# Fetching eight of the sixteen token pairs later, from another queue, in a fused early-fusion kernel

## The chip, the cores and the metric

The kernel runs on one core of one Trainium2 chip. The metric is the device time of one execution in microseconds (us), from three runs. A span is the time between the first and the last instruction of one profiled execution.

## The reference: what is computed

```python
h = tok(x)                                  # 32 images: 36 patches x 768 @ W_lin + b, class token, positions
h = concatenate([h, txt], axis=1)           # 37 + 128 = 165 tokens of width 256 per image
h = h + attn(layernorm(h))                  # 16 heads of 16, causal, every 4th key masked out
h = h + ffn(layernorm(h))                   # RMS norm, router over 8 experts, each takes the
                                            # top 660 of 5280 tokens, 256 -> 1024 gelu -> 256,
                                            # weighted, summed back, divided by the gate sums
```

The softmax subtracts a row maximum, so every score is computed twice: once to find the maximum of each query's row, and once, transposed, for the exponentials. All of it is float32; the products that need it are split into a high part and a low part (`q_hi`, `q_lo`).

## The kernel before, in words

There are three stages: attention over 32 images (until about 480 us), a search for the experts' thresholds, and eight experts. The change touches the first alone.

**Residual rows.** `H` holds all tokens in SBUF, as 16 pairs of images, 112 partitions x 768 floats (336 KB) each. `load_pair(queue, p)` fetches pair `p` with its text rows from the input `h0`; `place_cls` copies the class rows and `move_embedded(m)` the 36 patch rows of image `m` into it, once the load has landed. Loads are counted in five groups (`HP`: pairs 0; 1, 2; 3 to 5; 6 to 10; 11 to 15), and `place_cls(i)` waits for the whole of group `i`. Three pairs (0 to 2) are fetched by SyncE (SP) and thirteen by ScalarE (ACT): 3 to 6 at the start, 7 behind the first normalisation (L718), 8 to 15 in the rounds -3 to -1 (L732, L739).

**Rounds.** The five engines' programs are written by hand, each in its own order, and meet at semaphores. `ROUNDS` counts b from -4 to 33. In round b image b+2 gets queries, keys and values (`queries`, `keys`, `values`, L856 to L883), image b+1 its row maxima (`row_scores` L885, `row_max` L1288), image b its scores, exponentials and mix of values. The rounds before 0 are the ramp: TensorE (PE) runs them as `early_rounds` (L991), where the embedding products `embed(g)` (L842) stand between the first images' work.

**Between the engines.** ACT copies the queries out of PSUM as `q_hi` (L668); VectorE (DVE) makes `q_lo` and `k_lo` (`low_q`, `low_k`, L1277). Then SP packs an image (`pack`, L355): three copies of queries into `Qp` and six of keys into `Kp`, SBUF to SBUF, nine DMAs, all on SP's queue. `row_scores(n, 0)` on PE waits for all nine (`qk_packed`). Five row maxima later PE transposes them, DVE copies them (`copy_mT`, L1304), SP sends them into `Qp` (`pack_max`, L372), and `key_scores` (L924) may start. DVE is in order: in round -2 it makes the statistics of pair 1 (`ln1_stats_of(1)`, L1246), which wait for that pair's patch rows to land, and then `low_q(0)` and `low_k(0)`.

Of the kernel before, what the change touches and what calls it, by code (L numbers as in the profile page):

```python
# [53 lines left out]
NPAIR = B // 2  # L54
# [6 lines left out]
SMALL = 65  # L61
SK = 28
XP = ((0, 1), (1, 2), (2, 4), (4, 7), (7, NG))
HP = ((0, 1), (1, 3), (3, 6), (6, 11), (11, NPAIR))


# [59 lines left out]
def build(nc, xT, wl, h0, addrows, clsrows, minus, watt, vecs, rowv, w1, w2, const_f, const_b, out):  # L126
    ctx = ExitStack()
    with ctx:  # L128
# [135 lines left out]
        def bank(i):  # L264
            return ps_all[:, i, :]
# [4 lines left out]

        x_in = [sem(f"x_in{i}") for i in range(len(XP))]
        h_in = [sem(f"h_in{i}") for i in range(len(HP))]
# [58 lines left out]
        def load_x(queue, i):  # L331
            cols = slice(KF * XP[i][0] * GB * NP, KF * min(B, XP[i][1] * GB) * NP)
            queue.dma_start(xT_s[:, cols], xT[:, cols]).then_inc(x_in[i], 16)

        def load_pair(queue, p):
            i = [first <= p < last for first, last in HP].index(True)
            queue.dma_start(H4[0:HROWS, p], h0[:, p * RT:(p + 1) * RT, :]).then_inc(h_in[i], 16)


        @block.sync  # L340
        def _(sp):
            def place_cls(i):
                a, z = HP[i]
                sp.wait_ge(h_in[i], 16 * (z - a))
                sp.dma_start(H4[0:1, a:z, 0, :], cls_s[a:z, 0, :]).then_inc(cls_moved[i], 16)
                sp.dma_start(H4[T - A:T - A + 1, a:z, 1, :], cls_s[a:z, 0, :]).then_inc(cls_moved[i], 16)

            def move_embedded(m):
                g, j = divmod(m, GB)
                n, u = divmod(m, 2)  # L350
                p = 1 + u * (T - A)
                sp.wait_ge(emb_ready, g + 1)
                sp.dma_start(H4[p:p + NP, n, u, :], emb[j * NP:(j + 1) * NP, g, :]).then_inc(moved[n], 16)

            def pack(n):  # L355
                i, h = n % 3, n % 2
                if n >= 3:
                    sp.wait_ge(st_done, 4 * n - 8)
                else:
                    sp.wait_ge(pinit_done, (3, 5, 6)[n])  # L360
                sp.wait_ge(q_ready, n + 1)
                for row, src in enumerate((q_hi, q_hi, q_lo)):
                    sp.dma_start(Qp[32 * row:32 * row + 32, i, :, :].bitcast(F32), src[:, h, :, :].bitcast(F32)).then_inc(qk_packed[i], 16)
                sp.wait_ge(k_ready, n + 1)
                for row, src in enumerate((k_hi, k_lo, k_hi)):
                    for w in range(2):
                        sp.dma_start(Kp[32 * row + HD * w:32 * row + HD * w + HD, i, :, w, :].bitcast(F32),
                                     src[64 * w:64 * w + 64, h, :, :].bitcast(F32)).then_inc(qk_packed[i], 16)

            def pack_max(n):  # L370
                sp.wait_ge(mT_ready, n + 1)
                sp.dma_start(Qp[MROW:MROW + 2, n % 3, :, :].bitcast(F32), mT[0:NH, n % 2, :].bitcast(F32))\  # L372
                  .then_inc(m_packed[n % 3], 16)

            def store_h(p):
                sp.wait_ge(resid_ready, RT * p + RT)
                rows = out.rearrange("b t d -> (b t) d").rearrange("(n r q) d -> n q r d", r=RT, q=A)
                sp.dma_start(rows[p], H4[0:A, p]).then_inc(h_stored, 16)

            def store_xn(p):  # L380
                sp.wait_ge(xn2_ready, RT * p + RT)
                rows = xn_rows.rearrange("(n r q) d -> n q r d", r=RT, q=A)
                sp.dma_start(rows[p], xn2[0:A, p % 2]).then_inc(xn_stored[p % 2], 16)

            load_x(sp, 0)
            sp.dma_start(add_s[0:GB * NP], addrows).then_inc(add_in, 16)
            sp.dma_start(cls_s[:, :, :], clsrows).then_inc(add_in, 16)
            load_pair(sp, 0)
            load_x(sp, 2)
            load_x(sp, 3)  # L390
            load_pair(sp, 1)
            load_pair(sp, 2)
            load_x(sp, 4)

            for b in ROUNDS:
                n, u = divmod(b, 2)
                if 1 <= b < B - 6:
                    for i, (first, _) in enumerate(HP):
                        if b + 6 == 2 * first:
                            place_cls(i)  # L400
                    move_embedded(b + 6)
                if 0 <= b + 2 < B:
                    pack(b + 2)
                if b == -1:
                    place_cls(2)
                    for m in (4, 5, 6):
                        move_embedded(m)
                if 0 <= b + 1 < B:
                    pack_max(b + 1)
                if u == 1 and 0 <= n - 1 < NPAIR:  # L410
                    store_h(n - 1)
                if u == 1 and 0 <= n - 1 < NPAIR:
                    store_xn(n - 1)


            sp.wait_ge(h_stored, 16 * NPAIR)
            for e in range(2):
                sp.dma_start(W1[:, e, :, :], w1[e].rearrange("(k p) f -> p k f", p=128)).then_inc(w1_in[e], 16)
                sp.dma_start(W2[:, e, :, :], w2[e].rearrange("(k p) d -> p k d", p=128)).then_inc(w2_in[e], 16)
            def weights(e, u):  # L420
                sp.wait_ge(w1_split, KD * e - KD)
                apart(sp)
                sp.dma_start(W1[:, u, :, :], w1[e].rearrange("(k p) f -> p k f", p=128)).then_inc(w1_in[u], 16)
                sp.wait_ge(w2_split, KFF * e - KFF)
                apart(sp)
                sp.dma_start(W2[:, u, :, :], w2[e].rearrange("(k p) d -> p k d", p=128)).then_inc(w2_in[u], 16)

            with sp.Fori(1, NE // 2) as it:
                for u in range(2):
                    weights(2 * it + u, u)  # L430
            sp.wait_ge(scattered, 16 * NA * NE)
# [208 lines left out]
        def _(act):  # L640
# [83 lines left out]
            for b in ROUNDS:  # L724
                n, u = divmod(b, 2)
                if 0 <= b + 2 < B:
                    copy_q(b + 2)
                if 0 <= b < B:
                    exps(b, 0)
                if 0 <= b + 2 < B:  # L730
                    copy_k(b + 2)
                for p in {-3: (8, 9), -2: (10, 11), -1: (14, 15)}.get(b, ()):  # L732
                    load_pair(act, p)
                if 0 <= b < B:
                    exps(b, 1)
                if u == 0 and 0 < n + 2 < NPAIR:
                    ln1_apply(n + 2)
                if b == -2:
                    load_pair(act, 12)  # L739
                    load_pair(act, 13)  # L740
                if u == 1 and 0 <= n - 1 < NPAIR and b != B - 1:
                    ln2_apply(n - 1)
                if 0 <= b + 2 < B:
                    copy_v(b + 2)
                if 0 <= b < B:
                    exps(b, 2)
                if u == 1 and n + 2 < NPAIR:
                    copy_xnT(n + 2)
                if 0 <= b < B:
                    exps(b, 3)  # L750
                if b == B - 1:
                    ln2_apply(n - 1)
                if u == 1 and 0 <= n - 1 < NPAIR:
                    copy_xn2T(n - 1)
# [476 lines left out]
        def _(dve):  # L1231
# [6 lines left out]
            def embedded(g):  # L1238
                n = min(GB, B - g * GB) * NP
                dve.wait_ge(emb_mm, g + 1)  # L1240
                dve.tensor_tensor(emb[0:n, g, :], bank(g % 4)[0:n, 0:D], add_s[0:n, 0, :], ALU.add)\
                   .then_inc(emb_ready, 1)
# [39 lines left out]
            def low_q(n):  # L1282
                low_parts(n, bank(6), bq_s, q_hi, q_lo, TE, q_hi_ready, q_ready)

            def low_k(n):
                low_parts(n, bank(7), bk_s, k_hi, k_lo, S, k_hi_ready, k_ready)
# [36 lines left out]
            def round_of(b):  # L1323
                n, u = divmod(b, 2)
                has_q, has_r, has_s, has_p = -2 <= b < B - 2, -1 <= b < B - 1, 0 <= b < B, 0 <= n - 1 < NPAIR
                if b == -4:
                    embedded(1)
                if u == 0 and n + 2 < NPAIR:
                    ln1_stats_of(n + 2)
                if u == 1 and has_p:  # L1330
# [21 lines left out]
                    embedded(10)  # L1352
                if has_r:
                    row_max(b + 1, 0)
                if has_q and b != -1:
                    low_q(b + 2)
                if has_r:
                    row_max(b + 1, 1)
                if has_q and b != -1:
                    low_k(b + 2)  # L1360
                if has_r:
                    row_max(b + 1, 2)
# [367 lines left out]
```

## Time and profile before

| | |
|---|---|
| median of 3 runs | 842.74 us (842.41 to 844.98) |
| the profiled execution: time, span | 846.83 us, 844.9 us |
| PE busy | 743.7 us, 88% of the span |
| DVE, ACT, POOL busy | 567.9, 397.1, 383.2 us |
| chain that ended last: PE, DVE | 34%, 4% |
| DMA over the span | 82.37 MB, 97 GB/s |

PE is by far the busiest engine. The page's 40 slices of the span (21 us each) show where it is not: in the first (6 tenths), around 480 to 550 us, where the search runs on DVE, and at the end. The queue named q1 carries the DMAs that SP issues and q10 those of ACT; each DMA, from either queue, is spread over the same 16 DMA engines. "Idle before, releaser" names what ended an engine's idle time, and the time "to landing" of a DMA runs from its issue to the semaphore that tells of its end.

### The profile page before, as it was taken

How to read it: one execution, taken by the hardware profiler on the slowest of the kernel's cores; microseconds unless marked ns; L12 is line 12 of the kernel's file. 1: busy time of each engine (PE TensorE's matmuls, PEld its weight loads, DVE VectorE, ACT ScalarE, POOL GpSimd, SP SyncE). 2: the span in 40 equal slices, each digit the busy share in tenths (PEclk: the TensorE clock that was granted, in tenths of full speed). 3: DMA queues.
4: the chain of work that ended last, by engine and by line, in shares of the span. 5: the costliest groups of instructions: out<-in, count | busy, mean ns of one | idle time of the engine just before them, and what ended most of it. 6: DMA issues, size and time to landing. Idle time of an engine off the chain costs nothing. (4 is left out here: it accounts for less than half of the span.)

```text
span 844.9 us, 18782 instructions
## 1 busy us (share of the span) xinstructions
PE 743.7 (88%) x6840; PEld 673.4 (80%) x6840; DVE 567.9 (67%) x1343; ACT 397.1 (47%) x858; POOL 383.2 (45%) x534
## 2 busy tenths in 40 slices
PE   6959999999999999999998511389999999999994
PEld 4848888888888888888887411289999999999994
DVE  1326767767767768767666377876787787887461
ACT  0305445545445455455442256045647467375470
POOL 4214455455455455465453324213645437356334
PEclk9979999999999999999999655579999999999998
DMA  9975477475675665575651342002344443443122
GB/s 308 248 127 78 62 122 114 93 100 94 96 123 108 94 94 97 103 123 99 98 83 55 97 156 100 17 17 83 45 132 93 89 139 54 128 99 38 33 29 32
DMA packets 80583, 82.37 MB, mean 97 GB/s; under 512 B 35705, under 2 KB 73575, under 8 KB 80236
## 3 DMA queue, kind: packets, MB, share of 16 engines
q1 hardware_dynamic: 65964, 62.21, 37.3%
q0 software_dynamic: 11840, 11.12, 8.2%
q10 hardware_dynamic: 2688, 7.85, 3.6%
q8 instruction: 55, 0.90, 0.5%
q14 instruction: 36, 0.29, 0.1%
HBM read 34.59 MB, written 16.22 MB: 60 GB/s over the span
## 5 line engine op out<-in xcount | busy, mean ns | idle before, releaser
L626 POOL DMA_INDIRECT out<-r_arena x48 | 80.3, 1672 | 116.7 <-DVE r_arena L1591 104.7
L1298 DVE TENSOR_REDUCE mx<-ps_all 128x4 f32<-128x504 f32 (+1 forms) x160 | 104.9, 668 | 26.3 <-PE ps_all L901 24.9
L530 POOL TENSOR_SCALAR_AFFINE_SELECT r_arena<-r_arena 126x660 f32<-126x660 f32 x128 | 97.0, 768 | 52.1 <-ACT r_arena L690 52.1
L690 ACT ACTIVATE r_arena<-ps_all 126x660 f32<-126x660 f32 x128 | 92.2, 720 | 56.9 <-PE ps_all L924 55.5
L1309 DVE RECIPROCAL r_arena<-ps_all 128x165 f32<-128x165 f32 x64 | 76.1, 1189 | 57.5 <-PE ps_all L939 57.5
L901 PE MATMUL ps_all<-Kp,Qp 96*65 96x56 f32 (+1 forms) x512 | 92.4, 297 | 0.0
L1613 DVE TENSOR_TENSOR hT_lo<-r_arena,hT_hi 128x330 fp32r<-128x330 f32 x128 | 63.2, 500 | 41.8 <-ACT r_arena L803 41.6
L613 POOL DMA_INDIRECT xe<-xn_rows,r_arena x48 | 60.6, 1263 | 62.1 <-issue 35.7
L924 PE MATMUL ps_all<-Qp,Kp 98*126 98x166 f32 x512 | 84.3, 287 | 2.9 <-ACT r_arena L690 2.9
L801 ACT ACTIVATE hT_hi<-ps_all,vec_s 128x330 fp32r<-128x330 f32 x128 | 68.8, 538 | 37.7 <-PE ps_all L1166 36.4
L1166 PE MATMUL ps_all<-xeT_hi,W_hi 128*128 128x330 f32 x256 | 82.8, 323 | 1.8 <-DVE xeT_lo L1605 1.1
L1166 PE MATMUL ps_all<-xeT_lo,W_hi 128*128 128x330 f32 x256 | 81.9, 320 | 0.0
L1166 PE MATMUL ps_all<-xeT_hi,W_lo 128*128 128x330 f32 x256 | 81.6, 319 | 0.0
L1186 PE MATMUL ps_all<-hT_hi,W_hi 128*128 128x330 f32 x256 | 81.5, 319 | 0.0
L1186 PE MATMUL ps_all<-hT_hi,W_lo 128*128 128x330 f32 x256 | 80.6, 315 | 0.0
L1186 PE MATMUL ps_all<-hT_lo,W_hi 128*128 128x330 f32 x256 | 80.4, 314 | 0.0
L668 ACT ACTIVATE q_hi<-ps_all,vec_s 128x166 fp32r<-128x166 f32 x64 | 22.0, 395 | 122.8 <-PE ps_all L862 122.8
L924 PEld LDWEIGHTS ps_all<-Qp,Kp 98*126 98x126 f32 x512 | 68.8, 190 | 8.2 <-ACT r_arena L690 6.5
L901 PEld LDWEIGHTS ps_all<-Kp,Qp 96*65 96x65 f32 (+1 forms) x512 | 68.4, 170 | 5.6
L803 ACT ACTIVATE r_arena<-ps_all,vec_s 128x330 f32<-128x330 f32 x128 | 67.9, 530 | 0.0
L898 PE MATMUL ps_all<-cb 128*128 128x392 bf16 (+1 forms) x160 | 55.6, 347 | 13.4 <-DMA Kp<-k_hi 9.2
L939 PE MATMUL ps_all<-r_arena,V 126*32 126x165 f32 x1024 | 62.5, 316 | 1.1 <-POOL r_arena L530 1.0
(182 smaller groups left out, 1712.5 us busy)
## 6 DMA issues: line engine op xcount, KB each, us to landing
H<-w SPq DMA_DIRECT2D x16, 1024.0 KB, 5.7
Qp<-q_hi SPq DMA_DIRECT2D x64, 166.0 KB, 3.9
Kp<-k_hi SPq DMA_DIRECT2D x128, 63.0 KB, 4.1
Qp<-q_lo SPq DMA_DIRECT2D x32, 166.0 KB, 4.6
out<-H SPq DMA_DIRECT2D x16, 330.0 KB
xn_rows<-r_arena SPq DMA_DIRECT2D x16, 330.0 KB
H<-h ACTq DMA_DIRECT2D x13, 336.0 KB, 11.4
Kp<-k_lo SPq DMA_DIRECT2D x64, 63.0 KB, 4.0
```

The lines of the kernel that those rows point to most:

```text
L530: pool.affine_select(PT[0:S, g, :, :], PT[0:S, g, :, :], [[0, 4], [STEP - 1, T]], ALU.is_ge, 0.0, base=STEP - 2, channel_multiplier=-STEP) ...
L626: pool.indirect_dma_start(rows_out, bass.IndirectOffsetOnAxis(tok[0:A, e % NTB, a:a + 1], 0), yw[0:A, a, :], None, bounds_check=NTOK - 1, ...
L690: act.activation(PT[0:S, g, :, :].rearrange("p (k h) t -> p k h t", k=2), pair[:, :, :, 0:T], ACT.Exp, scale=float(HD) ** -0.5).then_inc(e ...
L801: act.activation(hT_hi[:, f, j * HALF:(j + 1) * HALF], bank(n % 4)[:, 0:HALF], ACT.Gelu, bias=b1_s[:, e, f:f + 1]).then_inc(gelu_done, 1)
L803: act.activation(h_raw[:, n % 4, :], bank(n % 4)[:, 0:HALF], ACT.Gelu, bias=b1_s[:, e, f:f + 1]).then_inc(gelu_done, 1)
L901: mm = pe.matmul(dst[0:rows, 2 * j * cols:2 * (j + 1) * cols].rearrange("p (w s) -> p w s", w=2), Qp[0:MROW, q, h, at_row:at_row + rows], ...
L924: mm = pe.matmul(dst[0:S, j * TE:(j + 1) * TE], Kp[0:MROW + 2, q, h, g % 2, :], Qp[0:MROW + 2, q, h, :], start=(j == 0), stop=(j == 1), sk ...
L1166: mm = pe.matmul(bank(n % 4)[:, 0:HALF], w[:, k, f * 128:(f + 1) * 128], x[:, k, cols], start=(i == 0), stop=(i == len(terms) - 1))
L1186: mm = pe.matmul(bank(4 + c)[:, 0:HALF], w[:, f, c * 128:(c + 1) * 128], h[:, f, cols], start=(i == 0), stop=(i == len(terms) - 1))
L1298: dve.tensor_reduce(dst, src, AX.X, ALU.max).then_inc(max_ready, 1)
L1309: dve.reciprocal(rS[:, c, :], bank(2 + c)[:, T:2 * T]).then_inc(rs_sum, 1)
L1613: dve.tensor_tensor(hT_lo[:, f, cols], h_raw[:, n % 4, :], hT_hi[:, f, cols].bitcast(F32), ALU.subtract).then_inc(h_ready, 1)
```

## The change

Two things change. Pairs 8 to 15 are no longer fetched by ACT in the rounds -3 to -1, but by SP: pair 8 in round -1, pairs 9 to 15 in the even rounds 0, 2, ... 12, each behind that round's `pack_max`. And on DVE `low_q(0)` and `low_k(0)` stand ahead of the statistics of pair 1. No wait is added or taken away.

```diff
+LATE = 8
@@ SyncE, in the loop over ROUNDS
                 if 0 <= b + 1 < B:
                     pack_max(b + 1)
+                if b == -1:
+                    load_pair(sp, LATE)
+                if u == 0 and 0 <= n and LATE + 1 + n < NPAIR:
+                    load_pair(sp, LATE + 1 + n)
                 if u == 1 and 0 <= n - 1 < NPAIR:
                     store_h(n - 1)
@@ ScalarE, in the loop over ROUNDS
-                for p in {-3: (8, 9), -2: (10, 11), -1: (14, 15)}.get(b, ()):
-                    load_pair(act, p)
...
-                if b == -2:
-                    load_pair(act, 12)
-                    load_pair(act, 13)
@@ VectorE, round_of(b)
+                if b == -2:
+                    low_q(0)
+                    low_k(0)
                 if u == 0 and n + 2 < NPAIR:
                     ln1_stats_of(n + 2)
...
-                if has_q and b != -1:
+                if has_q and b >= 0:
                     low_q(b + 2)
...
-                if has_q and b != -1:
+                if has_q and b >= 0:
                     low_k(b + 2)
```

DVE's program around round -2 (`st`, `mv`: the statistics of pair 1; `emb`: the embedding's rows), before:

```order
L1241 TENSOR_TENSOR emb<-ps_all,add_s 108x256
L1246 BN_STATS st<-H 110x6 x3
L1250 BN_AGGR mv<-st 110x2 x3
L1277 SCALAR_TENSOR_TENSOR q_lo<-ps_all,vec_s,q_hi 128x166 x2
L1277 SCALAR_TENSOR_TENSOR k_lo<-ps_all,vec_s,k_hi 128x126 x2
L1241 TENSOR_TENSOR emb<-ps_all,add_s 108x256 x2
```

and after:

```order
L1241 TENSOR_TENSOR emb<-ps_all,add_s 108x256
L1277 SCALAR_TENSOR_TENSOR q_lo<-ps_all,vec_s,q_hi 128x166 x2
L1277 SCALAR_TENSOR_TENSOR k_lo<-ps_all,vec_s,k_hi 128x126 x2
L1246 BN_STATS st<-H 110x6 x3
L1250 BN_AGGR mv<-st 110x2 x3
L1241 TENSOR_TENSOR emb<-ps_all,add_s 108x256 x2
```

The four instructions of the low parts have passed the six of the statistics.

SP's program from the end of round -1 to round 1 (`Qp<-mT` is `pack_max`, the other `Qp` and `Kp` rows are `pack`, `H<-emb` is `move_embedded`), before:

```order
L353 DMA H<-emb 36x256 x3
L372 DMA Qp<-mT 2x8x166
L363 DMA Qp<-q_hi 32x4x332 x2
L363 DMA Qp<-q_lo 32x4x332
L367 DMA Kp<-k_hi 16x8x126 x2
L367 DMA Kp<-k_lo 16x8x126 x2
L367 DMA Kp<-k_hi 16x8x126 x2
L372 DMA Qp<-mT 2x8x166
L353 DMA H<-emb 36x256
```

and after (all lines are one further down):

```order
L354 DMA H<-emb 36x256 x3
L373 DMA Qp<-mT 2x8x166
L338 DMA H<-h 112x768
L364 DMA Qp<-q_hi 32x4x332 x2
L364 DMA Qp<-q_lo 32x4x332
L368 DMA Kp<-k_hi 16x8x126 x2
L368 DMA Kp<-k_lo 16x8x126 x2
L368 DMA Kp<-k_hi 16x8x126 x2
L373 DMA Qp<-mT 2x8x166
L338 DMA H<-h 112x768
L354 DMA H<-emb 36x256
```

A load (`H<-h`) now stands behind a `pack_max` and ahead of the next round's work, here twice, and once more in each of the even rounds 2 to 12. On ACT the eight loads are gone from between the first activations, whose order stays.

## Rows read from the trace of the kernel before

**Rows 1.** Waits of PE, 0 to 110 us: us in total, times, longest.
```profile
PE ps_all L898 <- DMA Kp<-k_hi: 9.2, 1, 9.2
...
PE ps_all L881 <- DVE q_lo L1277: 0.7, 1, 0.7
```

**Rows 2.** Timeline of PE: start, us, line, operation, idle before and releaser.
```profile
44.50 2.75 PE L842 MATMUL ps_all<-r_arena 128*72 128x256 f32 x12
56.41 0.49 PE L898 MATMUL ps_all<-cb 128*128 128x392 bf16 x1 [9.16 <-DMA Kp<-k_hi]
56.44 0.88 PE L901 MATMUL ps_all<-Kp,Qp 96*128 96x252 f32 x2
...
65.28 0.88 PE L924 MATMUL ps_all<-Qp,Kp 98*126 98x166 f32 x4
...
88.50 0.34 PE L898 MATMUL ps_all<-cb 128*128 128x392 bf16 x1
88.54 0.54 PE L901 MATMUL ps_all<-Kp,Qp 96*128 96x252 f32 x2
```

**Rows 3.** Timeline of ACT and DVE, 28 to 45 us.
```profile
30.47 0.69 ACT L668 ACTIVATE q_hi<-ps_all,vec_s 128x166 fp32r<-128x166 f32 x2 [2.58 <-PE ps_all L862]
...
31.62 0.36 ACT L674 ACTIVATE k_hi<-ps_all,vec_s 128x126 fp32r<-128x126 f32 x1
...
32.54 1.08 DVE L1246 BATCH_NORM_STATS2 st<-H 110x6 f32<-110x256 f32 x3 [2.77 <-DMA H<-emb]
...
33.86 0.65 DVE L1277 SCALAR_TENSOR_TENSOR q_lo<-ps_all,vec_s,q_hi 128x166 fp32r<-128x166 f32 x2
...
37.58 0.36 ACT L681 ACTIVATE V<-ps_all 126x256 f32<-126x256 f32 x1
```

**Rows 4.** Timeline of SP, 30 to 90 us: start and length of the issues.
```profile
34.60 1.33 SPq L363 DMA_DIRECT2D Qp<-q_hi  x2
...
63.13 0.69 SPq L372 DMA_DIRECT2D Qp<-mT  x1
...
74.05 0.67 SPq L372 DMA_DIRECT2D Qp<-mT  x1
...
79.24 1.95 SPq L363 DMA_DIRECT2D Qp<-q_hi  x2
```

**Rows 5.** Landing of the last DMA that packs image 0, issued at 39.92 us.
```profile
DMA to landing us min/median/max: 16.4/16.4/16.4
```

**Rows 6.** The page's DMA issues: KB each, median us to landing.
```profile
Kp<-k_hi SPq DMA_DIRECT2D x128, 63.0 KB, 4.1
...
H<-h ACTq DMA_DIRECT2D x13, 336.0 KB, 11.4
```

**Rows 7.** DMA queues, 33.2 to 52.6 us: packets, MB, share of 16 engines.
```profile
q10 hardware_dynamic: 918, 2.45, 65.9%
q1 hardware_dynamic: 1565, 1.22, 42.1%
```

**Rows 8.** DMA queues, 27 to 31 us.
```profile
q10 hardware_dynamic: 364, 0.98, 97.3%
```

**Rows 9.** Windows: PE, PEld, DVE, ACT, POOL busy (count), PEclk, DMA share, GB/s.
```profile
56.00:66.00 10.00, 9.45 (x42) 7.79 (x43) 4.99 (x12) 1.50 (x4) 1.44 (x5) 0.51 0.11 27
...
438.00:441.00 3.00, 2.52 (x25) 2.07 (x23) 1.32 (x3) 1.90 (x5) 2.90 (x5) 1.00 1.11 141
441.00:445.00 4.00, 4.00 (x66) 2.93 (x64) 1.39 (x2) 1.05 (x3) 0.77 (x1) 0.57 0.42 83
```

**Rows 10.** Waits of PE, 65 to 215 us.
```profile
PE ps_all L898 <- DVE mx L1298: 1.0, 6, 0.2
```

**Rows 11.** Waits of SP, 65 to 215 us.
```profile
SPq L361 <- DVE q_lo L1277: 47.9, 12, 5.8
```

**Rows 12.** The loads that SP issues at the start: ns per issue.
```profile
L337 SPq DMA_DIRECT2D H<-h x3: 478/481/640, 2.1 to 4.5; - x3
```

**Rows 13.** Landing of the last DMA that packs image 3, issued at 85.11 us.
```profile
DMA to landing us min/median/max: 2.7/2.7/2.7
```

## The prediction, on record before the changed kernel ran

> **What bounds the kernel now.** I read PE's waits of the first 110 us first, since PE is busy for 88% of the span and an edit of the ramp can only pay where PE stands still. One wait stands out: the first row scores, for 9.2 us, on a key copy of `pack(0)`; the wait for the low queries is 0.7 us [rows 1]. The timeline places it: PE ends its embedding products at 44.50 + 2.75 = 47.25 and starts `row_scores(0, 0)` at 56.41 [rows 2]. Next I asked why the copies land so late. SP issues the nine of `pack(0)` from 34.60 on [rows 4], and the last, issued at 39.92, lands 16.4 us later, at 56.3 [rows 5], where the kernel's median for such a copy is 4.1 us [rows 6]. Third view, the queues: from 33.2 to 52.6 us ACT's queue q10 moves 2.45 MB with 65.9% of the 16 DMA engines' time and SP's q1 1.22 MB with 42.1% [rows 7]. What ACT has queued then are token pairs of 336 KB; 2.45 MB is seven of them, which is what is left of pairs 8 to 15. So PE waits for copies that share the engines with text rows nobody needs for many rounds. DMA is the bound of this stretch, and PE of what follows: from 65 to 215 us its row scores wait 1.0 us in all for DVE's maxima, and for no copy [rows 10].
>
> **Part 1, the loads leave the ramp.** Eight loads of 336 KB go. Alone, ACT's queue moved 0.98 MB in 4 us, 245 GB/s [rows 8], so the eight are 8 x 344 KB / 245 GB/s = 11.2 us of all engines, taken from the stretch in which `pack(0)` and `pack(1)` stand. What of it is on the path? With q10 empty from about 33 us, the copies have the engines for themselves. The nearest row for that is `pack(3)`, whose last copy, alone in the queue, lands 2.7 us after its issue [rows 13]; the median is 4.1 [rows 6]. `pack(0)` would then land at 39.9 + 4.1 = 44.0, and 2.7 us sooner by part 2, about 41.4. PE is busy until 47.25, so the whole wait of 9.16 us goes, with some 6 us to spare. The other bound, that they land as slowly as before, is rival C. What is late next is PE itself: its embedding products. ACT's eight issues cost or gain nothing: ACT stands waiting for PE around them, as the 2.58 us ahead of `q_hi` show [rows 3].
>
> The Trainium skill ("DMA: Bandwidth & Descriptors", "Queues, rings and completion order") says that each DMA engine round-robins between the queue rows it has work for, a packet at a time. By that rule small copies lose most against big rows, and the trace agrees, the shares of q10 and q1 being as above; the sum would come out the same.
>
> **Part 2, the low parts first.** `q_hi` is complete at 30.47 + 0.69 = 31.16 and `k_hi` at 31.62 + 0.36 = 31.98, but DVE stands before the statistics of pair 1 until 32.54 and makes `q_lo` only at 33.86 [rows 3]. Moved ahead, `q_lo` starts at about 31.25 and ends at 31.9; `k_lo` ends near 32.6. SP's first issue, which follows `q_lo`'s end by 0.1 us [rows 3, 4], comes at 31.95 instead of 34.60: 2.65 us earlier. PE's 0.7 us wait for `q_lo` [rows 1] goes too. It buys nothing at the end: the next queries wait for the copy of V out of the same bank (`query_bank`), which ends at 37.94 [rows 3] and stands on ACT behind the normalisation of pair 1. That hangs on the statistics, which now start 0.1 us later (32.65 for 32.54). So the embedding products end at 47.25 + 0.1 = 47.35. This part alone pays at most its 2.65 us, if the copies land as slowly as before; with part 1 it is inside the spare 6 us and costs 0.1. Were the queries free of V's copy, the 0.7 us would count: 0.6 is its other end.
>
> **Part 3, the clock.** While PE stood still its granted clock fell, and from 56 to 66 us it was 0.51 of full, 1.2 instead of 2.4 GHz [rows 9]. The stretch from the first row scores to the first `key_scores`, 56.41 to 65.28 = 8.87 us [rows 2], is a chain of score tiles, maxima, transposes, `mT` and `pack_max`. At full clock a tile's two products take 0.54 us for 0.88 [rows 2], 0.39 less of each microsecond. On the chain lie the first tile, the ends of the others (the rest is under the maxima), the last, small tile and the transposes, by my estimate 3.6 us of PE: 3.6 x 0.39 = 1.4 us. Bounds: 0, if the clock falls in this sparse stretch all the same, as it did at 441 us behind a stretch with PE busy 2.52 of 3 us [rows 9]; 1.4, if it holds. I take 0.9, nearer to holding: PE now comes into this stretch busy instead of from 9 us of rest.
>
> `pack_max(0)` needs SP free: `pack(1)` starts when `pack(0)` is issued and the next low queries are there, about 41, and takes as long as `pack(0)`, from 34.60 to 39.92 + 0.6, 5.9 us; class and patch rows take some 4 us, to about 51. The first `mT` came 63.13 - 56.41 = 6.7 us behind the first row scores [rows 2, 4], so it is due at 47.35 + 6.7 - 1.4 = 52.7 or later: SP is there 1.7 us before it.
>
> **Part 4, the loads in the rounds.** Each costs SP one issue, 0.48 us [rows 12]. Behind it stand `move_embedded` and the next `pack`, and who waits for those is DVE (statistics a round or more later) and PE. Between a `pack_max` (74.05 + 0.67 = 74.7) and the next `pack` (79.24) SP has 4.5 us with one patch copy in it, the rest a wait for `q_lo` [rows 4]; over 150 us these waits are 47.9 us in 12, 4.0 each [rows 11]. So the issue is free. The transfer: 344 KB / 245 GB/s = 1.4 us [rows 8], from about 75.3, over by about 78 with its latency, ahead of the next `pack` at 79.2. If a part falls upon a pack, little is there to catch it: `pack(3)` lands at 85.11 + 2.7 = 87.8 and PE needs it at 88.50 [rows 2, 13], 0.7 us of slack. Bounds for one load: 0, and 1.4 - 0.7 = 0.7 us if all of the transfer delays a pack. Seven loads lie in rounds: 0 to 4.9 us. I take 0.3 in all. The data is needed late: pair 10, the last of its group, is issued in round 2 and first waited for in round 6.
>
> **The sum.** 9.16 - 0.1 + 0.9 - 0.3 = 9.7 us less. From the profiled execution, 846.83 us (span 844.9 and 1.9 around it), 837.1. The median of the runs is 4.1 us below the profiled time, so 842.74 - 9.7 = 833.0. A shift of the ramp is passed on whole: behind it PE is the bound up to the end of attention, and the search and the experts begin when attention ends. What may change there is the clock: it fell and rose several times near the end of attention [rows 9], and where a fall lies against the work may change by itself; the three runs before spread by 2.6 us.
>
> **The rivals.**
> *A, the forecast*: the gap closes and the rounds keep their pace. 833.0; its own range 830.5 to 835.5. For it: rows 7 and 8 add up, and the cover is 6 us.
> *B, the rounds pay*: the loads' transfers fall upon packs of 0.7 us slack. With 0.7 us for each of seven, 833.0 + 4.6 = 837.6. Against it: SP's 4 us waits, into which a transfer of 1.4 us fits.
> *C, the copies are slow by themselves*, not by q10: the last copy still takes 16.4 us to land. Then only part 2 counts: 842.7 - 2.65 = 840.1. For it: q1 had 42.1% of the engines for 1.22 MB, so the small rows are dear. Against it: in the rounds the same copies land in 4.1 us.
> *D, slower*: a load ahead of a pack in SP's own queue holds the whole queue. If it took its 11.4 us of the ramp [rows 6], a load issued at 74.7 would land at 86.1, and the pack behind it 86.1 - 79.2 = 6.9 us later than now, less 0.7 of slack: 6.2 x 7 = 43 us, and 833 + 43 = 876. It decides from 9.7 / 7 = 1.4 us of delay beyond the slack for each load. Against it: the 11.4 us were a place behind up to four other loads; nothing is ahead of these but a 10 KB copy.
> The skill ("DMA: Bandwidth & Descriptors", "Issuing engines are not separate DMA queues") speaks against this change: transfers from all engines end up on the same 16 DMA engines, and another issuer only saves issue time. By it the move from ACT to SP wins nothing, and only the later time can. I share that view; it gives D its chance, since in the rounds q1 alone is busy.
>
> **How the numbers follow.** A 0.80, B 0.10 (with anything from 836 to 840), C 0.06, D 0.04. The lower end of the range: full clock and free loads give 832.2, and 2.6 us of spread below it, 829.5. The upper end takes in most of B: 837.5. Outside lie C, D, and parts of A and B, about 0.15. A measurement here can tell 0.3%, 2.5 us, from no change. Faster by more than that needs under 840.2: all of A and B and half of C, 0.93. Within: 0.03. Slower: D, 0.04.
>
> **What would show it.** Right: PE's wait before its first row scores is under 1 us, and those start near 47.4 us; the last copy of `pack(0)` is issued near 37.3 and lands by 43; q10 carries nothing after about 34 us; the first `key_scores` stands near 55; the start of every later round is 9 to 11 us earlier, so that row scores 3 start near 79; each load in the rounds lands within 4 us. Wrong: PE's row scores wait for `Kp` copies in odd rounds (B), the 16.4 us landing stays (C), or the shift at 79 us has shrunk by 400 us (B, D). I would be wrong on the clock if it is below 1 between 48 and 55 us.

## The result and the profile after

The changed kernel takes 834.06 us (median of 4 runs, 832.7 to 834.9); beside it on the same chip the kernel before took 842.69 us (4 runs, 842.41 to 844.98). The ratio is 0.9881 with a 95% interval of 0.9848 to 0.9914. A second series gave 834.15 against 843.23 us, ratio 0.9884 (0.9862 to 0.9905). Forecast were 833.0 us and a range of 829.5 to 837.5.

PE's waits of the first 110 us, after (us in total, times, longest), to be laid beside [rows 1]:

```profile
PE ps_all L842 <- DMA r_arena<-wl: 6.4, 1, 6.4
PE ps_all L842 <- DMA r_arena<-xT: 1.6, 1, 1.6
PE ps_all L924 <- DMA Qp<-mT: 1.4, 2, 1.2
...
PE ps_all L862 <- ACT V L686: 0.7, 1, 0.7
```

The wait of 9.2 us for a key copy is gone, and no wait for `Kp` is left. The first two rows, waits for the embedding's inputs, stood there before too (6.4 and 1.4 us). The wait of 1.2 us for `pack_max(0)` is new: PE now comes to the first key scores before that copy has landed. The 0.7 us for `q_lo` have become 0.7 us for the copy of V. PE's timeline (start, us, line, operation), to be laid beside [rows 2]; the last row starts the row scores of image 29, near the end of attention:

```profile
44.61 2.75 PE L842 MATMUL ps_all<-r_arena 128*72 128x256 f32 x12
47.20 0.33 PE L898 MATMUL ps_all<-cb 128*128 128x392 bf16 x1
...
54.28 0.67 PE L924 MATMUL ps_all<-Qp,Kp 98*126 98x166 f32 x4 [1.24 <-DMA Qp<-mT]
...
77.76 0.34 PE L898 MATMUL ps_all<-cb 128*128 128x392 bf16 x1
...
410.12 0.34 PE L898 MATMUL ps_all<-cb 128*128 128x392 bf16 x1
```

The first row scores follow the embedding products at once. They stand 9.21 us earlier (56.41 to 47.20), the first key scores 11.0 us (65.28 to 54.28), row scores 3 10.74 us (88.50 to 77.76). The same row scores 29 of before:

```profile
420.92 0.34 PE L898 MATMUL ps_all<-cb 128*128 128x392 bf16 x1
```

420.92 - 410.12 = 10.80 us. Of the 11.0 us at the first key scores 0.3 are lost by row scores 3; from there on nothing is paid back or added in 26 rounds. SP's timeline shows the earlier issues and the loads (`H<-h`), beside [rows 4]:

```profile
32.09 1.91 SPq L364 DMA_DIRECT2D Qp<-q_hi  x2
...
37.46 1.25 SPq L368 DMA_DIRECT2D Kp<-k_hi  x2
...
52.15 0.69 SPq L373 DMA_DIRECT2D Qp<-mT  x1
52.88 0.40 SPq L338 DMA_DIRECT2D H<-h  x1
...
63.36 0.39 SPq L338 DMA_DIRECT2D H<-h  x1
...
68.42 2.05 SPq L364 DMA_DIRECT2D Qp<-q_hi  x2
```

The last copy of `pack(0)`, issued at 38.11, now lands like this, for the 16.4 us of [rows 5]:

```profile
DMA to landing us min/median/max: 2.4/2.4/2.4
```

and the queues (packets, MB, share of the 16 engines' time) from 33.2 to 52 us, for [rows 7]:

```profile
q1 hardware_dynamic: 2748, 1.91, 61.0%
...
q10 hardware_dynamic: 8, 0.02, 0.6%
```

ACT's queue is all but empty. SP's carries 1.91 MB for 1.22, since its own work comes earlier. Over the whole kernel the loads on SP's queue land in a median of 3.9 us, for 11.4 on ACT's in [rows 6]:

```profile
H<-h SPq DMA_DIRECT2D x11, 336.0 KB, 3.9
```

Last, the clock: a window from 47 to 55 us (busy time of PE, PEld, DVE, ACT, POOL with counts, then PEclk, DMA share and GB/s), for the 0.51 of [rows 9]:

```profile
47.00:55.00 8.00, 6.01 (x45) 4.71 (x44) 5.19 (x13) 1.59 (x5) 1.94 (x6) 1.00 0.42 68
```

The granted clock is full. The stretch from the first row scores to the first key scores is 54.28 - 47.20 = 7.08 us, for 8.87 before.

### The profile page after: what moved, and what is told of

It reads as the page before. It is cut to its first block and busy times, and to the rows that moved or that the text cites. A ratio compares the mean times of both kernels' runs of the same rounds, so it can differ in the third digit from the quotient of the medians.

```text
span 831.0 us, 18782 instructions
## 1 busy us (share of the span) xinstructions
PE 739.2 (89%) x6840; PEld 670.2 (81%) x6840; DVE 566.7 (68%) x1343; ACT 397.2 (48%) x858; POOL 384.1 (46%) x534
## 5 line engine op out<-in xcount | busy, mean ns | idle before, releaser
L901 PE MATMUL ps_all<-Kp,Qp 96*65 96x56 f32 (+1 forms) x512 | 90.6, 293 | 0.0
L801 ACT ACTIVATE hT_hi<-ps_all,vec_s 128x330 fp32r<-128x330 f32 x128 | 68.9, 538 | 38.2 <-PE ps_all L1166 37.3
L939 PE MATMUL ps_all<-r_arena,cf 126*32 126x165 f32 x1024 | 60.5, 309 | 0.0
```

The source lines that it names most:

```text
L801: act.activation(hT_hi[:, f, j * HALF:(j + 1) * HALF], bank(n % 4)[:, 0:HALF], ACT.Gelu, bias=b1_s[:, e, f:f + 1]).then_inc(gelu_done, 1)
L901: mm = pe.matmul(dst[0:rows, 2 * j * cols:2 * (j + 1) * cols].rearrange("p (w s) -> p w s", w=2), Qp[0:MROW, q, h, at_row:at_row + rows], ...
L939: mm = pe.matmul(dst, lhs, PT[0:S, 2 * c + w, j, :], start=(w == 0 and part == 0), stop=(w == 1), skip_group_check=True)
```

## The experiments

**The kernel before once more** (`e0_before`), unchanged, for a second profile of it.

> The kernel before, unchanged, profiled once more. Its ramp is the same in every execution: first row scores at 56.4 us, row scores 29 at 420.9. If the difference between the profiled pair (846.83 and 832.70, 14.1 us) and the medians (842.69 and 834.06, 8.6 us) is the clock at the end of attention and in the search, this profile's time is near 842.7 and its falls of the clock between 435 and 475 us lie elsewhere or are fewer; rival: the profiled execution was slow in the rounds, and row scores 29 stand elsewhere than at 420.9.

Measured: 846.36 us; the runs of before in this series have a median of 843.74 (839.59 to 848.1, 23 runs). Row scores 29:

```profile
422.73 0.34 PE L898 MATMUL ps_all<-cb 128*128 128x392 bf16 x1
```

The time is much like that of the first profile, and not the 842.7 expected, but for another reason: row scores 29 were 1.8 us later (422.73 for 420.92). The first row scores had come at 56.61 and the first key scores at 65.53, only 0.2 us later than in the first profile; then the clock stayed at half to 69.2 us, for 65.7 there. So what the fallen clock costs differs between executions, and the shift at row scores 29 lies between 10.4 and 12.6 us for the two profiles of either kernel. From row scores 29 to the end of the span it took 844.5 - 422.7 = 421.8 us for 844.9 - 420.9 = 424.0. So two profiled executions are compared at places in the rounds, not by their ends.

**The loads moved, the low parts left** (`e1_loads_only`):

```diff
-                if b == -2:
-                    low_q(0)
-                    low_k(0)
...
-                if has_q and b >= 0:
+                if has_q and b != -1:
                     low_q(b + 2)
```

and the same for `low_k`.

> The change without the low parts ahead of the statistics. Theory (the loads do it all): pack(0) is issued from 34.6 on and its last copy lands near 43, still ahead of PE's 47.2; first row scores at 47.1 to 47.3, row scores 29 at 410.1 as in the full change, time 834. Rival (the earlier low parts are needed): row scores 2.6 us later, time 836.5.

Measured: 833.28 us (832.67 to 836.8, 6 runs), ratio 0.9886 (0.9854 to 0.9917). The first issue of `pack(0)`, and row scores 0 and 29:

```profile
34.54 1.33 SPq L364 DMA_DIRECT2D Qp<-q_hi  x2
```
```profile
47.03 0.33 PE L898 MATMUL ps_all<-cb 128*128 128x392 bf16 x1
...
410.19 0.34 PE L898 MATMUL ps_all<-cb 128*128 128x392 bf16 x1
```

The copies are issued 2.45 us later than in the changed kernel (34.54 for 32.09), the last lands at 39.8 + 3.7 = 43.5, and PE is not there until 47. Row scores 29 are 0.07 us from the changed kernel's. The loads' move is the whole gain.

**The low parts moved, the loads left** (`e2_low_only`, and once more, unchanged, as `e2b_low_only`):

```diff
+                if b == -2:
+                    low_q(0)
+                    low_k(0)
...
-                if has_q and b != -1:
+                if has_q and b >= 0:
                     low_q(b + 2)
```

> The kernel before with the low parts ahead of the statistics alone. Theory: the copies of pack(0) are issued 2.65 us earlier but still share the engines with the pairs; PE's wait shrinks by 0 to 2.65 us, time 840 to 842.7. Rival (the order on DVE does it): the wait goes, time 834.

Measured: 843.52 us (835.5 to 847.84, 12 runs), ratio 0.9999 (0.9974 to 1.0023): no gain, where I had expected 840 to 842.7. The profile, though, was of the one run of 835.5 us, in which the last copy landed 9.0 us behind its issue at 39.86 and row scores 0 began at 49.02. So it was profiled again:

> The same kernel as in e2_low_only, profiled once more. That profile had the last copy of pack(0) at 48.9 us and a time of 835.5, while its other eleven runs took 840.4 to 847.8. If that execution was an exception, this one shows the copy near 54 and 840 to 845 us; if not, the copy is near 49 again and the gain of about 7 us in the ramp has to be lost somewhere behind it.

Measured: 843.94 us. The first issue of `pack(0)`, the landing of its last copy (issued at 38.0), and row scores 0:

```profile
31.86 1.34 SPq L363 DMA_DIRECT2D Qp<-q_hi  x2
```
```profile
DMA to landing us min/median/max: 18.3/18.3/18.3
```
```profile
56.50 0.48 PE L898 MATMUL ps_all<-cb 128*128 128x392 bf16 x1 [8.80 <-DMA Kp<-k_hi]
```

Issued 1.9 us sooner (38.0 for 39.92), the last copy lands 1.9 us slower (18.3 for 16.4), at 56.4 as before: in these two executions the issue time made no difference, and by the median of twelve runs part 2 alone is worth nothing. In both, ACT's queue is all but empty from 52 us on, and the engines spend the last 4 us of PE's wait almost wholly on SP's own copies of `pack(0)` and `pack(1)`, which had piled up behind the loads. The kernel before, 53 to 56.4 us:

```profile
q1 hardware_dynamic: 818, 0.46, 106.6%
```

The one run of twelve went otherwise. There the clock had fallen at 16.9 us, and ACT came to its loads some 1.8 us later (33.2 and 37.95 us for 31.4 and 36.1). From 37 to 41 us SP's queue moved 0.56 MB, for 0.31 in `e2b_low_only`, and the copies were through at 48.9 us. That fits a wait made by ACT's loads; which of the two, the fallen clock or the later loads, did it, no run sets by itself.

**PE kept busy in the gap** (`e3_busy_gap`): the kernel before with 52 idle products on a bank that nothing reads, ahead of the first row scores.

```diff
                 pe.wait_ge(cb_in, 16)
+                for _ in range(52):
+                    pe.matmul(bank(4)[:, 0:392], ident_b, kb("mask_big"), start=True, stop=True)
                 row_scores(0, 0, None)
```

> The kernel before with 52 products of no use into a free PSUM bank, ahead of the first row scores, so that PE is busy for most of its wait. Theory (1.4 us of the gain is the clock): first row scores stay at 56.4 us, the granted clock stays 1.0, and the first key scores follow after 7.5 us instead of 8.9, so that row scores 29 stand 1.4 to 1.8 us earlier than 420.9. Rival (that stretch is latency and not clock): they stay at 420.9 within 0.3.

Measured: 842.58 us (840.92 to 844.25, 10 runs), ratio 0.9988 (0.9968 to 1.0008). Windows, and the first key scores:

```profile
48.00:56.00 8.00, 7.59 (x46) 4.27 (x44) 0.00 (x0) 0.00 (x0) 0.00 (x0) 1.00 1.10 168
56.00:66.00 10.00, 7.62 (x59) 6.43 (x59) 6.18 (x16) 2.79 (x7) 2.69 (x7) 1.00 0.18 35
```
```profile
63.48 0.67 PE L924 MATMUL ps_all<-Qp,Kp 98*126 98x166 f32 x4 [1.22 <-DMA Qp<-mT]
```

With the gap filled the clock stays full, and key scores 0 stand at 63.48 for 65.28: 1.8 us earlier behind copies that came no earlier (row scores 0 at 56.41 in both). That is the clock's term by itself, and the 7.1 us from row scores to key scores are those of the changed kernel. Row scores 29 come 2.0 us earlier, where 1.4 to 1.8 were expected:

```profile
418.94 0.34 PE L898 MATMUL ps_all<-cb 128*128 128x392 bf16 x1
```

The 0.2 us more are gained behind the first key scores, where the kernel before runs at half clock until 65.7 us. The total tells a gain of 1.0 us (1 - 0.9988 of 843), with an interval that just reaches no change; the place in the rounds tells it plainly.

**The loads ahead of a `pack`** (`e4_ahead_of_pack`): in the same rounds, but between the wait for `q_lo` and the nine copies, so that no idle time of SP covers them.

```diff
                 sp.wait_ge(q_ready, n + 1)
+                late(n - 2)
                 for row, src in
```

> The change, with each late load issued one step later: not behind the maxima of an even round but directly ahead of the nine copies of the next pack, behind its wait for the low queries. Theory (the 4 us in which SP waits are what hides the loads): each load's 1.4 us of transfer now delays a pack whose slack is 0.7 to 1.4 us; summed over images 3, 5, ... 15 PE loses 2.4 us, or 5.2 with the issue of 0.4 us on top. Row scores 29 then stand at 412.5 to 415.5 instead of 410.1, time 836.5 to 839. Rival (a transfer of 336 KB is too small to be felt wherever it stands): 410.1 and 834.

Measured: 833.13 us (829.28 to 837.48, 4 runs), ratio 0.984 (0.9781 to 0.9898). SP in round 1, the landing of `pack(3)`'s last copy, and row scores 29:

```profile
67.96 0.33 SPq L338 DMA_DIRECT2D H<-h  x1
68.33 1.27 SPq L371 DMA_DIRECT2D Qp<-q_hi  x2
```
```profile
DMA to landing us min/median/max: 2.8/2.8/2.8
```
```profile
409.81 0.34 PE L901 MATMUL ps_all<-cb 128*128 128x392 bf16 x1
```

With the load straight ahead of it, the last copy of `pack(3)` still lands in 2.8 us, and row scores 29 come 0.3 us earlier than in the changed kernel. The loss of 2.4 to 5.2 us that my theory wanted is not there. The last of the nine copies is issued 5.6 us behind the load (67.96 to 73.6), and by then a load of some 1.4 us of transfer should be through; the loads land in 3.7 to 4.3 us.

The early rounds say more. The ramp is the same in both kernels (row scores 0 at 47.20 and 47.21, key scores 0 at 54.28), but key scores 1 stand at 65.47 us here and at 65.94 in the changed kernel, where PE waits for `pack_max(1)`:

```profile
65.94 0.68 PE L924 MATMUL ps_all<-Qp,Kp 98*126 98x166 f32 x4 [0.19 <-DMA Qp<-mT]
```

Row scores 3 come at 77.20 for 77.76. So the place that I had taken for the dear one is the cheaper by 0.6 us there, and by 0.3 at row scores 29.

**The loads in the rounds, from ACT** (`e5_act_late`), behind the last activations of the same rounds:

```diff
                 if 0 <= b < B:
                     exps(b, 3)
+                if b == -1:
+                    load_pair(act, LATE)
+                if u == 0 and 0 <= n and LATE + 1 + n < NPAIR:
+                    load_pair(act, LATE + 1 + n)
```

> The change, with the eight loads in the same rounds but issued by ACT behind its last exponentials. Theory (only the time of the loads counts, not the queue): as the change, row scores 29 within 0.3 us of 410.1, time 834. Rival (SP's queue and its order are needed): packs land later, their slack of 0.7 us goes, 836 or more.

Measured: 835.82 us (831.5 to 838.5, 4 runs), ratio 0.9873 (0.9808 to 0.9938). PE in round 1, then its waits for `pack_max` from 54 to 204 us:

```profile
67.32 0.67 PE L924 MATMUL ps_all<-Qp,Kp 98*126 98x166 f32 x4 [1.36 <-DMA Qp<-mT]
```
```profile
PE ps_all L924 <- DMA Qp<-mT: 3.5, 4, 1.5
```

Later is what counts: nearly all of the gain is there with ACT as issuer. But ACT comes to the load at 61.61 us, while the copies of `pack(2)` are being issued, and the last of them lands in 4.8 us, for 3.7. PE waits 3.5 us for `pack_max` in four waits, for 1.4 in two, and row scores 29 stand at 411.66, 1.5 us later. Of these 1.5 us 1.3 are there at row scores 3 (79.05 for 77.76): the loss lies with the loads of the rounds -1 and 0, and those of the later rounds cost 0.2 or 0.3 us together. "No difference" was 1.5 us off; the place in the round that the issuer gives is what differs, though no run moves ACT's loads within the round.

**All loads on SP at the start** (`e6_sp_early`): no load in the rounds.

```diff
             load_x(sp, 4)
+            for p in range(LATE, NPAIR):
+                load_pair(sp, p)
```

> The other half: the eight loads on SP's queue, but all at the start, behind the last part of x. Theory (a queue is worked off in order, the engines' 11.2 us for the loads are spent before or among the copies of pack(0)): its last copy lands at 45 to 48 us, row scores 0 at 47 to 49, time 834 to 837. Rival (only a later load helps, since the bytes are the same): the copies land near 56 as before, time 843.

Measured: 845.58 us (841.97 to 847.31, 10 runs), ratio 1.0002 (0.9977 to 1.0027). PE's wait, the landing of `pack(0)`'s last copy (issued at 40.5), and the queues from 33.2 to 52.6 us:

```profile
PE ps_all L896 <- DMA Kp<-k_hi: 7.4, 1, 7.4
```
```profile
DMA to landing us min/median/max: 14.9/14.9/14.9
```
```profile
q1 hardware_dynamic: 2253, 3.13, 94.6%
q10 hardware_dynamic: 242, 0.64, 14.1%
```

The same bytes in the same stretch from SP's queue cost nearly the same: PE waits 7.4 us, for 9.2, and row scores 29 stand at 419.48, 1.4 us of the change's 10.8 earlier. Another queue is no cure. Here the Trainium skill ("DMA: Bandwidth & Descriptors", "Issuing engines are not separate DMA queues") says that transfers share the 16 engines whoever starts them, and that another issuer saves its issue time only; this run agrees. My figures of 45 to 48 us for the last copy and 47 to 49 for row scores 0 were wrong (55.4 and 55.57). I had priced the loads ahead of the copies and not the copies. Small rows are dear by themselves, as the queue shows from 46 to 50 us, when the loads are through and it carries copies of the packs:

```profile
q1 hardware_dynamic: 759, 0.57, 116.6%
```

That is 0.57 MB in 4 us at a full share, where loads moved 0.98 MB [rows 8]; and `pack(0)` and `pack(1)` together are some 1.8 MB, by the sizes of their copies.

**Four loads at once** (`e7_four_at_once`): pairs 9 to 12 in round 0, 13 to 15 in round 2.

```diff
-                if u == 0 and 0 <= n and LATE + 1 + n < NPAIR:
-                    load_pair(sp, LATE + 1 + n)
+                if b in (0, 2):
+                    for p in (range(LATE + 1, LATE + 5), range(LATE + 5, NPAIR))[n]:
+                        load_pair(sp, p)
```

> The change, with four loads behind the maxima of round 0 and three behind those of round 2, a dose four times as large. Theory (SP's wait covers 4.5 us): four transfers take 5.6 us, from 63.4 to about 70, and pack(3), issued from 68.4 on, lands 1.5 to 3 us later than 77.1, so that row scores 3 lose 1 to 2.5 us against 77.8; the three of round 2 have longer cover and cost 0 to 0.5. Row scores 29 at 411 to 413. Rival (the transfers are not felt at all): 410.1.

Measured: 833.23 us (829.01 to 838.6, 4 runs), ratio 0.9839 (0.9781 to 0.9898). The four issues, the next pack's first, and row scores 3:

```profile
65.13 1.85 SPq L338 DMA_DIRECT2D H<-h  x4
...
70.17 1.27 SPq L364 DMA_DIRECT2D Qp<-q_hi  x2
```
```profile
79.41 0.34 PE L899 MATMUL ps_all<-cb 128*128 128x392 bf16 x1
```

The loads take 3.7 to 6.1 us to land; the last copy of the pack behind them lands in 2.5. Row scores 3 are 1.65 us later than in the changed kernel, but row scores 0 were 1.8 later already (48.98; the clock fell at 17 us in this execution), and row scores 29 are 1.75 later (411.87). So 1.3 MB at this place delays nothing more than one load does there. My theory, 1 to 2.5 us, fell.

**Two more pairs late** (`e8_six_late`): pairs 6 and 7 too, three loads in round -1, and none of the two at the start.

```diff
                 if b == -1:
-                    load_pair(sp, LATE)
+                    for p in (LATE - 2, LATE - 1, LATE):
+                        load_pair(sp, p)
...
-            for p in range(3, 7):
+            for p in range(3, 6):
                 load_pair(act, p)
...
-            load_pair(act, 7)
```

> The change, with pairs 6 and 7 moved too: three loads behind the maxima of round -1. Theory (with the eight loads gone the ramp is bound by PE's embedding products): row scores 0 stay within 0.3 us of 47.2, row scores 29 at 410.1, time 834. Rival (DMA still bounds the ramp): row scores 0 one to three us earlier, 831 to 833.

Measured: 833.62 us (831.4 to 834.41, 4 runs), ratio 0.9885 (0.9864 to 0.9906). PE's window from 14 to 22 us:

```profile
14.00:22.00 8.00, 6.15 (x21) 4.62 (x22) 1.63 (x7) 0.00 (x0) 0.70 (x2) 0.79 1.04 321
```

The same window of the changed kernel:

```profile
14.00:22.00 8.00, 6.42 (x30) 5.11 (x30) 2.47 (x9) 0.00 (x0) 0.60 (x4) 1.00 1.04 330
```

No gain over the changed kernel: from 33 us on PE waited for no key copy there either. The ramp in the profile is 1.9 us later (row scores 0 at 49.08), with a clock of 0.79 in this window; it fell in `e7_four_at_once` and `e2_low_only` too. What these three have in common stands just ahead of the fall: PE waits 2.1 to 2.3 us for a part of x at about 15 us. In the ten profiles whose clock held there, this wait was 0.9 to 1.7 us (`e9_ramp` has none). So the rival, that row scores 0 would come earlier, did not come true, and "within 0.3 us of 47.2" missed by the clock.

**Pairs 3 to 5 and the weights later as well** (`e9_ramp`), so that the first patch rows come sooner:

```diff
-            act.dma_start(W_s[:, :, :, :], watt).then_inc(w_in, 16)
...
+            act.dma_start(W_s[:, :, :, :], watt).then_inc(w_in, 16)
             act.dma_start(cb[:, :], const_b).then_inc(cb_in, 16)
-            for p in range(3, 6):
-                load_pair(act, p)
...
             ln1_apply(0)
+            for p in range(3, 6):
+                load_pair(act, p)
```

on top of the edit before.

> As e8_six_late, and ahead of it ACT fetches the attention weights (1 MB) behind the small tables instead of ahead of them, and pairs 3 to 5 only behind the first normalisation. Theory (what PE still waits for in the ramp is a part of x, 1.4 us at 15.5 us, which shares the engines with the weights): that part lands earlier, the wait goes, row scores 0 at 45.8 to 46.5, time 832.7 to 833.5. Rival (the copy of V behind the statistics of pair 1, or DVE, then holds PE): 47.2 and 834.

Measured: 834.98 us (831.42 to 841.44, 5 runs), ratio 0.9902 (0.9881 to 0.9924). PE behind the patch rows of pair 0:

```profile
27.17 1.33 PE L852 MATMUL ps_all<-cf,xn 110*128 110x110 f32 x6 [3.61 <-ACT xn L710]
```

Missed. The part of x that PE waits for in the changed kernel lands in 12.9 us for 15.4, but the patch rows of pair 0 take 7.7 for 5.9, and PE waits 3.6 us for the normalised rows; in this wait the clock falls (half from 26.4 to 33.2 us) and row scores 0 come at 51.26. Of this run's two edits I can't say which did it.

**The changed kernel once more** (`e10_after_again`), unchanged.

> The change itself, again, beside the two above. Row scores 0 at 47.2 and 29 at 410.1 us, or both 1.7 us later where the clock falls near 17 us, as in two profiles so far; time 832 to 836. If the rounds keep their pace, all of the variation between executions lies in the first 20 us and from 430 us on.

Measured: 834.15 us (832.97 to 836.71, 4 runs), ratio 0.9884 (0.9862 to 0.9905). Row scores 0 and 29 stand at 47.56 and 410.57, within 0.5 us of the first profile's; from row scores 29 to the end it took 424.4 us, for 420.9 in the first. No version here clearly beats the change by its time; `e4_ahead_of_pack` has row scores 29 some 0.3 to 0.8 us earlier (409.81), which a median of four runs can't tell.

## Why the prediction was right, step by step

**Part 1** held. Row scores 0 were due at 47.35 and came at 47.20. `pack(0)` was due to be through by 41.4 and landed at 38.11 + 2.4 = 40.5. That the copies were slow by ACT's loads (and not by themselves, rival C) is shown by `e1_loads_only` from one side, and by `e6_sp_early` from the other: loads from another queue in the same stretch bring the wait back. One thing my account left out: ACT's loads are through at 52 us, and PE waits to 56.4. They hold the copies back until those of `pack(1)` are queued as well, and the engines then work both off. I had also read the turns that the two queues take, a packet at a time, from the shares of [rows 7]. The shares alone don't show them; the packet counts of `e6_sp_early` do (last section). Only the issue of `pack(0)` was off by 0.8 us (its last at 38.11, forecast 37.3), since two of the copies took 1.2 and 0.8 us to issue; the cover of 6 us took it.

**Part 2** held. DVE's rows, beside [rows 3]:

```profile
31.32 0.69 DVE L1277 SCALAR_TENSOR_TENSOR q_lo<-ps_all,vec_s,q_hi 128x166 fp32r<-128x166 f32 x2 [1.42 <-ACT q_hi L673]
32.66 1.07 DVE L1246 BATCH_NORM_STATS2 st<-H 110x6 f32<-110x256 f32 x3
```

`q_lo` starts at 31.32 (forecast 31.25), the statistics 0.1 us later. PE's wait moved to V's copy with its whole 0.7 us. Worth alone: nothing, where I had allowed up to 2.65 us; `e2b_low_only` shows copies issued 1.9 us sooner into that traffic that land no sooner.

**Part 3** is the term that was mis-sized. Forecast were 0.9 us, at most 1.4; measured are 8.87 - 7.08 = 1.8 us, and `e3_busy_gap` gives 1.8 by itself. The direction was right. My 1.4 was a count of 3.6 us of PE on the chain from row scores to key scores, times 0.39, with the rest of PE's work "under the maxima". The traces show otherwise. From the first row scores to the end of the transposes of the maxima, before and after:

```profile
56.40:62.75 6.35, 6.25 (x29) 4.88 (x29) 3.36 (x5) 0.89 (x2) 0.00 (x0) 0.50 0.11 29
```
```profile
47.20:51.76 4.56, 3.81 (x31) 2.87 (x30) 3.56 (x6) 0.89 (x2) 0.37 (x2) 1.00 0.45 60
```

At half clock PE is busy for 6.25 of 6.35 us and waits for nothing: the chain is all PE, and none of it is hidden under the maxima. Among its work are six transposes of the next normalised rows (L852), which my list doesn't name. At full clock its 6.25 us become 3.81, 2.4 less (6.25 x 0.39 = 2.4), and now PE does wait for DVE's maxima, 0.36 and 0.38 us. 2.4 less these 0.7 are 1.7 of the 1.8 us. SP was free at 50.8 (51), and `pack_max(0)` was issued at 52.15, 0.5 us sooner than the "52.7 or later", by the same term.

**Part 4**: the size was near, 0.5 us for 0.3, and the reason was wrong. Each load takes 0.4 us to issue (the last 1.0) and lands in 3.3 to 4.0 us. From the first key scores to row scores 3 the changed kernel takes 23.5 to 23.6 us in all three profiles that have its loads (`after`, `e1_loads_only`, `e10_after_again`), and 22.9 in `e3_busy_gap`, at full clock with no load there, and in `e4_ahead_of_pack`. From row scores 3 to 29 all kernels take 332.4 to 332.7 us. So the later loads are free, and some 0.5 us are lost once, at key scores 1, which wait for `pack_max(1)`. I had it that SP's waits of 4 us make room for the transfers, and that one which falls upon a pack costs up to 0.7 us. `e4_ahead_of_pack` puts each upon a pack and costs nothing, and `e7_four_at_once` puts four together and costs no more than one. As I read it, the nine issues of a pack cover a load ahead of them, since the last copy is issued 5.6 us behind it; no run takes that cover away. `pack_max` has no such cover, and the waits of `e5_act_late` are for it. The placement chosen, behind the `pack_max`, is therefore not the cheapest one here. But `e8_six_late` and `e9_ramp` have a load in the same place behind `pack_max(1)` and take 22.9 to 23.0 us, so what decides over the 0.5 us stays open.

**The sum**: 10.8 us in the rounds, for 9.7: 9.2 for the wait (forecast 9.06), 2.1 for the clock up to row scores 3 by `e3_busy_gap` (0.9), less 0.5 for the loads (0.3). The medians of the two series fell by 8.6 and 9.1 us, each with an interval that holds 10.8 (0.9848 of 842.69 is 12.8 us less). That the measured 834.06 lies so near the forecast 833.0 is partly luck: the gain in the rounds was 1.1 us larger than forecast and the fall of the median 1.1 us smaller, so that two misses offset each other. The two profiled executions differ by 14.1 us, of which 10.8 are the change; the other 3.3 us are nearly all how the end fell out (844.9 - 420.9 = 424.0 against 831.0 - 410.1 = 420.9). Over all profiles this stretch took 418 to 426 us, kernels of both kinds mixed (before and its variants 420.4 to 424.0, the changed kernel 420.9 and 424.4). The 65 us from row scores 29 on (busy times as above, then PEclk), `e4_ahead_of_pack` with 425.9 us:

```profile
409.81:474.81 65.00, 52.99 (x509) 43.11 (x508) 32.53 (x72) 21.49 (x41) 24.55 (x42) 0.83 0.37 74
```

and `e8_six_late` with 418.1 us, which does as many products with 3.6 us less of PE busy:

```profile
411.55:476.55 65.00, 49.39 (x511) 40.71 (x511) 35.37 (x77) 22.07 (x43) 28.20 (x44) 0.85 0.43 94
```

The longer of these two has more of it at half clock. But the clock of this window doesn't put all ends in order: it is 0.87 in the changed kernel's first profile, with 420.9 us, and 0.84 both in `e1_loads_only`, with 420.7, and in the kernel before, with 424.0. That falls of the clock make the difference is not shown, and what sets where they come stays open.

**The rivals.** B fell: no copy of a pack is waited for in the rounds, only `pack_max(1)` for 0.2 us, and even loads that fall upon packs are free. C fell with the landing of 2.4 us, though it was right that small rows are dear: from 44 to 48 us the changed kernel's copies alone fill the engines with 0.50 MB. D fell: behind a load on SP's queue a pack lands in 2.5 to 2.8 us. The 11.4 us of [rows 6] were indeed other loads.

## What to carry to other kernels

When a wait is for a small DMA that takes several times its usual landing, look for what else the 16 DMA engines move in that stretch: data needed late belongs out of it. Here a later time helped, another queue did not, and an earlier issue of the small copies gained nothing by the median. When you price the DMA that you move, look for the transfer that the waiting engine waits for last: here a load ahead of a row of nine issues cost nothing, and what little was lost came at the copy that is issued alone and waited for at once. When you price a clock, count which engine the chain hangs on at either clock; here PE alone at half, PE and DVE in turn at full. And where the ends of executions scatter by more than the effect, read its size at a fixed place in the loop, before the scatter.

## What the runs showed of the hardware

- Idle PE cost more than the idle time: behind 9.2 us of waiting the clock was at half, and the stretch to the first key scores took 1.8 us longer. Idle products in the gap gave this back in `e3_busy_gap`. The clock was full again at 65.7 us in one profile of the kernel before and at 69.2 in the other, which cost that one 1.5 us more by row scores 3.
- The clock fell in the ramp of some executions and not of others: near 17 us in `e2_low_only`, `e7_four_at_once` and `e8_six_late`, which put row scores 0 at 48.98 to 49.08, against 47.20 and 47.56 in the changed kernel. In these three PE had just waited 2.1, 2.1 and 2.3 us for a part of x; in the ten profiles whose clock held there, 0.9 to 1.7.
- A copy of 63 KB in short rows landed 16.4 us after its issue beside 2.45 MB of text rows, and in 2.4 us without them. Issued 1.9 us sooner into the same traffic, it took 1.9 us longer to land.
- Short rows fill the engines with fewer bytes: 0.50 MB in 4 us of `pack(1)`'s copies alone (changed kernel, 44 to 48 us, a share of 119%), against 0.98 MB of loads (27 to 31 us, 97.3%).
- While both queues had work, they moved equal numbers of packets: 462 on SP's and 463 on ACT's from 10 to 20 us of `e6_sp_early`, 388 and 386 from 20 to 30.
- The time of an issue on SP varies: 0.6 us for most copies, 0.8 and 1.2 us for two copies of `pack(0)` at 33 to 35 us in the changed kernel, and 2.1 and 2.5 us for two copies of `pack(1)` in the kernel before, at 42 to 46 us, while those of `pack(0)` had not landed. What sets it no run separates.
